# The sparse layer's counts are turned by transposing DMAs from SyncE instead of by TensorE

## The reference, cut to what matters

```python
inter = xf @ c1_w.T @ c2_w.T                      # 1792 columns
blk = inter.reshape(B * T, n_blocks, SPARSITY)    # 56 blocks of 32
idx = jnp.argmax(blk, axis=-1) + jnp.arange(0, INTER, SPARSITY)
h = jax.nn.relu(jnp.einsum('bkm,bm->bk', w1[idx], xf))
out = jnp.einsum('bk,bkm->bm', h, w2t[idx])
```

## Time and profile before

| what | value |
|---|---|
| median of 3 runs | 672.27 us (671.7 to 673.28) |
| the profiled execution's own time | 671.89 us |
| its span in the profile | 670.1 us |
| TensorE matmul busy | 638.2 us (95%), 3078 instructions |
| VectorE busy | 449.9 us (67%) |
| ScalarE busy | 213.8 us (32%) |
| GpSimd busy | 233.0 us (35%) |
| DMA | 40.66 MB, mean 61 GB/s |
| first layer's chunks (TensorE's bodies), about | 45 to 126, 145 to 226, 246 to 327, 346 to 428 us |

### The profile page before, as it was taken

One profiled execution on the slowest core, in us unless ns is written; L12 is line 12 of the kernel. 1 busy time (PEld: TensorE's weight loads), 2 busy tenths in 40 slices (PEclk: granted clock), 3 DMA queues, 4 the chain that ended last, 5 costly groups with the idle time before them and its releaser, 6 DMA issues.

```text
span 670.1 us, 8639 instructions
## 1 busy us (share of the span) xinstructions
PE 638.2 (95%) x3078; PEld 515.8 (77%) x3078; DVE 449.9 (67%) x716; ACT 213.8 (32%) x379; POOL 233.0 (35%) x185
## 2 busy tenths in 40 slices
PE   2599999999999999999999999999999999999997
PEld 2478788778788778788777788787878878887887
DVE  6977875597664597664597786664856667485633
ACT  2423333412122412122411233654146126413610
POOL 1516555360000360000390343464514342342441
PEclk9899999999999999999999999999999999999999
DMA  8940000040000040000052110013021013002001
GB/s 237 405 172 1 0 1 0 24 166 1 0 1 0 23 167 0 0 0 0 19 213 108 63 49 15 16 49 126 32 102 56 1 47 141 0 31 80 17 23 41
DMA packets 19535, 40.66 MB, mean 61 GB/s; under 512 B 2032, under 2 KB 2416, under 8 KB 18864
## 3 DMA queue, kind: packets, MB, share of 16 engines
q1 hardware_dynamic: 19504, 40.25, 16.9%
HBM read 31.85 MB, written 8.39 MB: 60 GB/s over the span
## 4 chain that ended last, share of the span: by engine, by line
PE 85%; DVE 8%; issue 3%; POOL 1%; ACT 1%; DMA 1%; SPq 0%; DVEq 0%; POOLq 0%; ACTq 0%
PE bank L410 76%; PE bank L344 2%; PE bank L1154 2%; PE bank L1135 1%; DVE counts L882 1%; DVE eq L872 1%; DVE seg_top L870 1%; PE bank L1286 1%; DVE ws_lo L935 1%; PE bank L1117 1%; PE bank L1249 1%; DMA x_tile<-in_x 1%; DVE h_lo L906 1%; POOL g_tile L390 1%; DVE ws_raw L930 1%
## 5 line engine op out<-in xcount | busy, mean ns | idle before, releaser
L410 PE MATMUL bank<-w_hi_t,h_hi 128*128 128x512 f32 x224 | 93.6, 418 | 1.5 <-DVE h_lo L906 1.5
L708 ACT ACTIVATE h_hi<-h 128x512 fp32r<-128x512 f32 x56 | 35.4, 632 | 176.4 <-DVE h L897 176.4
L882 DVE TENSOR_TENSOR_SCAN counts<-restart,eq 128x512 bf16<-128x512 bf16 (+1 forms) x64 | 87.4, 1365 | 2.0
L410 PE MATMUL bank<-w_lo_t,h_hi 128*128 128x512 f32 x224 | 87.9, 392 | 0.0
L410 PE MATMUL bank<-xT_hi,w_hi_t 128*128 128x512 f32 x224 | 87.6, 391 | 0.0
L410 PE MATMUL bank<-w_hi_t,h_lo 128*128 128x512 f32 x224 | 87.5, 390 | 0.0
L410 PE MATMUL bank<-xT_lo,w_hi_t 128*128 128x512 f32 x224 | 87.2, 389 | 0.0
L410 PE MATMUL bank<-xT_hi,w_lo_t 128*128 128x512 f32 x224 | 87.2, 389 | 0.0
L870 DVE TENSOR_REDUCE seg_top<-bank 128x16 f32<-128x512 f32 (+1 forms) x64 | 39.6, 619 | 67.8 <-PE bank L1135 67.8
L390 POOL TENSOR_TENSOR g_tile<-g_tile,s_tile 128x512 f32<-128x512 f32 x31 | 43.7, 1408 | 94.3 <-DVE g_tile L919 49.4
L376 POOL TENSOR_TENSOR rstd<-mean_var,eps 128x4 f32<-128x4 f32 x8 | 1.6, 202 | 173.9 <-DVE mean_var L370 173.9
(11 more groups left out here) (185 smaller groups left out, 1304.8 us busy)
## 6 DMA issues: line engine op xcount, KB each, us to landing
w_raw<-in_w SPq DMA_DIRECT2D x28, 256.0 KB, 9.5
x_res<-in_x SPq DMA_DIRECT2D x4, 1024.0 KB, 8.0
mid_state<-g_tile SPq DMA_DIRECT2D x16, 256.0 KB, 2.0
x_tile<-mid_state SPq DMA_DIRECT2D x4, 1024.0 KB, 7.4
x_res<-mid_state SPq DMA_DIRECT2D x4, 1024.0 KB, 5.5
out<-g_tile SPq DMA_DIRECT2D x15, 256.0 KB, 2.0
x_tile<-in_x SPq DMA_DIRECT2D x3, 1024.0 KB, 5.4
b_raw<-in_lora_b SPq DMA_DIRECT2D x2, 1024.0 KB, 4.9
```

What stands on the lines that cost most here:

```text
L410: last = nc.tensor.matmul(dst, a, b, start=(start and n == 0), stop=(stop and n == len(mms) - 1))
L708: nc.scalar.activation(h_hi[:, it % 2, :], h[:], ACT.Copy).then_inc(h_hi_done, 1)
L882: nc.vector.tensor_tensor_scan(counts[:, p % 2, tt, 0:PW[p]], restart[:, 0:PW[p]], eq[:, 0:PW[p]], 0.0, ALU.mult, ALU.add).then_inc(sel_co ...
```

## The change

The four transposes of each iteration leave TensorE. Behind each select's scan, SyncE waits for the count and issues one transposing DMA, from `counts` to a tile `first` in SBUF with the columns on its partitions. One DMA turns one row tile of a whole piece (128 rows by 512 or 256 columns of bf16), so there are 16 in a chunk and 64 in all, in place of 224 transposes. The mask reads `first` from SBUF, and waits at iterations 0, 4, 8 and 12 for the four DMAs of its piece. `counts` keeps one buffer per row tile, `first` has two. In the head each select now stands directly behind its own `s` product, and the fourth select moves from the body (behind up product 0) into the head. In SyncE's program the loads take places between the DMAs of the pieces.

```diff
+            def turn(c, p, tt):
+                sp.wait_ge(sel_count, c * NSEL + p * TT + tt + 1)
+                sp.sem_inc(turns, 1)
+                sp.dma_start_transpose(first[:, p % 2, 0:PW[p] // P, rows(tt)], counts[:, tt, 0:PW[p]])\
+                    .then_inc(ld_first[tt], 16)
...
             def chunk(c, source, last):
+                for tt in range(TT):
+                    turn(c, 1, tt)
                 sp.wait_ge(xT_tr, c * TT + TT)
                 sp.dma_start(x_tile[:], source).then_inc(ld_x, 16)
                 sp.dma_start(x_res[:], x_rows[c]).then_inc(ld_res, 16)
                 if last:
                     sp.wait_ge(s0_done, CH * TT)
                     sp.dma_start(wqkv_raw[:], wqkv).then_inc(ld_wqkv, 16)
                     sp.dma_start(a_raw[:], a_w).then_inc(ld_wqkv, 16)
                     sp.wait_ge(s_biased, CH * TT)
                     sp.dma_start(bias_a[:], bo.rearrange("(a n) -> a n", a=1).to_broadcast([P, D])).then_inc(ld_bo, 16)
+                for tt in range(TT):
+                    turn(c, 2, tt)
+                if last:
                     sp.wait_ge(up_done, (CH - 1) * IT + KD + 1)
                     sp.dma_start(base_raw[:], base_w).then_inc(ld_base, 16)
                     sp.dma_start(wo_raw[:], wo).then_inc(ld_base, 16)
...
+                for tt in range(TT):
+                    turn(c, 3, tt)
+                    if last and tt == 0:
+                        next_b(0)
+                if last:
+                    next_b(1)
+            def rows_out(c, place, to_next):
+                for tt in range(TT):
+                    if to_next:
+                        turn(c + 1, 0, tt)
+                    store_row(c, place, tt)
...
             def select_count(c, p, tt):
-                if tt == 0 and p >= 2:
-                    dve.wait_ge(first_tr, c * IT + 4 * (p - 1))
+                turned = c * PIECES + p
+                if not (isinstance(turned, int) and turned == 0):
+                    dve.wait_ge(ld_first[tt], turned * 16)
...
-                    dve.wait_ge(first_tr, c * IT + it + 1)
-                    nc.vector.scalar_tensor_tensor(h[:], first, 1.0, h[:], ALU.is_equal, ALU.mult).then_inc(h_masked, 1)
+                    if it % 4 == 0:
+                        for tt in range(TT):
+                            dve.wait_ge(ld_first[tt], (c * PIECES + it // 4 + 1) * 16)
+                    nc.vector.scalar_tensor_tensor(h[:], first[:, it // 4 % 2, it % 4, :], 1.0, h[:],
+                                                   ALU.is_equal, ALU.mult).then_inc(h_masked, 1)
...
-            def transpose_counts(c, it):
-                pe.wait_ge(sel_count, c * NSEL + (it // 4 + 1) * TT)
-                if it:
-                    pe.wait_ge(h_masked, c * IT + it)
-                for tt in range(TT):
-                    last = nc.tensor.transpose(first[:, rows(tt)], counts[:, it // 4 % 2, tt, rows(it % 4)], ident_bf[:])
-                last.then_inc(first_tr, 1)
...
-                s_product(c, 0)
-                s_product(c, 1)
-                select(c, 0, 0)
-                s_product(c, 2)
-                select(c, 0, 1)
-                s_product(c, 3)
-                select(c, 0, 2)
+                for tt in range(TT):
+                    s_product(c, tt)
+                    select(c, 0, tt)
```

More of the change, by code:

```diff
@@ L101, in block_mask_ffn_then_attention_lora_kernel @@
         ident = few.take("ident", [P, P])
-        ident_bf = few.take("ident_bf", [P, P], BF16)
         restart = few.take("restart", [P, BANK], BF16)
@@ L192, in block_mask_ffn_then_attention_lora_kernel @@
         eq = span_t.take("eq", [P, BANK], BF16)
-        counts = span_t.take("counts", [P, 2, TT, BANK], BF16)
+        first = span_t.take("first", [P, 2, TT, S], BF16)
+        counts = span_t.take("counts", [P, TT, BANK], BF16)
         h = span_t.take("h", [P, S])
@@ L268, in block_mask_ffn_then_attention_lora_kernel @@
         sel_count = sem("sel_count")
-        first_tr = sem("first_tr")
+        turns = sem("turns")
+        ld_first = [sem(f"ld_first_{tt}") for tt in range(TT)]
         up_done = sem("up_done")
@@ L416, in block_mask_ffn_then_attention_lora_kernel @@
         on = g_tile[:, 0, 2 * P:3 * P]
-        c2_f = counts[:].bitcast(F32).rearrange("p a t n -> p (a t n)")[:, 0:INTER]
+        c2_f = first[:].bitcast(F32).rearrange("p a t n -> p (a t n)")[:, 0:INTER]
         C2_PARTS = [slice(0, BANK), slice(BANK, INTER)]
@@ L422, in block_mask_ffn_then_attention_lora_kernel @@
         mask_bank = banks[5]
-        first = banks[7][:].bitcast(BF16)[:, 0:S]
         NSEL = PIECES * TT
@@ L463, in _, with store_row, next_b @@
                 sp.dma_start(bqkv_col[:], bqkv.rearrange("(j p) -> p j", p=P)).then_inc(ld_l1_small, 16)
+            def turn(c, p, tt):
[3 more added lines that the diff above has]
+                    .then_inc(ld_first[tt], 16)
+            def store_row(c, place, tt):
+                sp.wait_ge(rows_done, c * TT + tt + 1)
+                sp.dma_start(place[:, tt, :], g_tile[:, tt, :]).then_inc(st_rows, 16)
+            def next_b(i):
+                part = slice(i * KE // 2, (i + 1) * KE // 2)
+                sp.wait_ge(down_done, (CH - 1) * IT + part.stop)
+                sp.dma_start(b_raw[:, part, :], lora_b[:, part, :]).then_inc(ld_b[i], 16)
             def chunk(c, source, last):
+                for tt in range(TT):
+                    turn(c, 1, tt)
                 sp.wait_ge(xT_tr, c * TT + TT)
@@ L494, in _ @@
             sp.sem_inc(g_free, 1)
+            for tt in range(TT):
+                turn(0, 0, tt)
             with sp.Fori(0, CH - 1) as c:
                 chunk(c, x_rows[c + 1], False)
+                rows_out(c, mid_rows[c], True)
             chunk(CH - 1, mid_rows[0], True)
+            rows_out(CH - 1, mid_rows[CH - 1], False)
             def chunk(c, source):
@@ L525, in _ @@
             gp.memset(ident[:], 0.0).then_inc(consts_gp, 1)
-            gp.memset(ident_bf[:], 0.0).then_inc(consts_gp, 1)
             gp.memset(neg_half[:], -0.5).then_inc(consts_gp, 1)
             gp.memset(eps[:], EPS).then_inc(consts_gp, 1)
-            gp.wait_ge(consts_gp, 4)
-            for m in (ident, ident_bf):
-                gp.affine_select(out=m[:], in_=m[:], compare_op=ALU.not_equal, fill=1.0, base=0,
-                                 pattern=[[-1, P]], channel_multiplier=1).then_inc(consts_gp, 1)
+            gp.wait_ge(consts_gp, 3)
+            gp.affine_select(out=ident[:], in_=ident[:], compare_op=ALU.not_equal, fill=1.0, base=0,
+                             pattern=[[-1, P]], channel_multiplier=1).then_inc(consts_gp, 1)
             gp.sem_inc(s_free, TT)
@@ L886, in head @@
                 t_rest(c)
-                for tt in range(TT - 1):
+                for tt in range(TT):
                     select(c, 0, tt)
             def body(c, last):
-                select(c, 0, TT - 1)
                 for it in range(IT):
@@ L1178, in body @@
                     up_product(c, 0)
-                    select(c, 0, 3)
                 for it in range(1, IT + 1):
```

12 lines of the change are left out of this document (3 added, 9 removed).

## The result

The changed kernel takes 695.15 us (median of 4 runs, 694.8 to 697.05) beside 672.58 for the kernel before: ratio 1.0342, 95% interval 1.0321 to 1.0363, so 22.6 us slower. The direction was forecast; the forecast of 683.0 lies 12 us under the time, and the stated range holds it. The profiled execution took 697.05 us with a span of 694.9, 24.8 more than before.

The account below looks back on a forecast made before the run. TensorE, with 85% of the chain of waits, was taken to bound the kernel. Terms -13.5 + 1.5 + 2.3 + 2 + 7.0 + 7.2 + 1.7 + 3 = +11.2 on 671.89 gave 683.1 us; range 668 to 702.

Parts of the forecast that it names:

- term 3: Chunk 0: later opening, +2.3 us, and the mask with both operands in SBUF held by GpSimd, +2 us.
- Term 4: Last chunk: wqkv and a load behind a turn, so h_lo is late for down product 4, +7.0 us.
- Term 6: Last chunk: second half of b loads behind the turn of (3, 3), wanted in iteration 12, +1.7 us.
- Term 7: TensorE's clock at half speed after the long waits of terms 4 and 5, +3 us.
- Term 1: TensorE's transposes removed: 0.30 us for each of 45 groups, -13.5 us.
- Term 2: Openings of chunks 1 to 3: the turn's latency makes each about 0.5 us longer, +1.5 us.
- L: The turn, from a scan's end over SyncE's wait, issue and landing to the mask's start; taken as 4.0 us.
- rival (b): Openings: a turn as short as a store, L = 2.0, 8 us better, 675 us; chance 0.14.
- Term 5: Last chunk: base and wo load behind the turn of (2, 3), making TensorE wait in iteration 7, +7.2 us.
- Opening of the last chunk: Part of Term 2: one of three openings forecast about 0.5 us longer.
- What counted as nothing: No cost from x_tile and x_res of chunks 0 to 2, or turns of pieces 1 to 3 within an iteration.
- Rival (c): Last chunk: moved weights are hidden, terms 4 to 7 (18.9 us) fall away, faster at 663 us; chance 0.12.

Follow-up runs that it names:

- e7: Changed kernel with the last chunk's loads ahead of the turns and chunk 0 alone turned by TensorE into PSUM: 662.6 us.
- e1: Changed kernel with the last chunk's loads moved back ahead of the turns in SyncE's program: 673.0 us.
- e11: Kernel before with only the opening's order changed, each select right behind its s product: 667.8 us.
- e4: Kernel before with its mask reading unturned counts in SBUF instead of the turned counts in PSUM; TensorE still transposes: 682.7 us.
- e5: Changed kernel with its mask reading a PSUM bank filled once, not the counts; DMAs and waits stay: 680.4 us.
- e8: Kernel before with wqkv, a, bias, base, wo and b issued as late as in the changed one, x_tile and x_res early: 681.0 us.
- e9: Kernel before with every load of the last chunk, x_tile and x_res included, issued as late as in the changed kernel: 687.9 us.
- e2: Changed kernel with only the turns of piece 1 moved behind x_tile, x_res, wqkv, a and bias: 683.8 us.
- e3: Changed kernel with only the turns of piece 2 moved behind base and wo: 685.4 us.
- e12: As e7, with a second transposing DMA of 128x128 into an unread tile ahead of each turn: 674.4 us.

## Why the prediction came out as it did

The sign was right, and the mechanisms that the sum names all occurred; only half of the loss was forecast. The step that failed is term 3, chunk 0. It let GpSimd take 0.3 us from the mask in each of some eight iterations, +2 in all, and put the body's end at nothing. The runs showed a mask held to the end of GpSimd's instruction, 7.1 us over seven iterations, and 3 more at the body's end: +10. Terms 4, 6 and 7 were mis-sized as well: 9.0, 5.1 and 5.6 us where 7.0, 1.7 and 3 stood. Terms 1 and 2 were too pessimistic.

By chunks, chunk 0 was 9.3 us worse than forecast and the last one 8.0 worse, while chunks 1 and 2 together were 3.4 better. Without this last error the time would stand at about 698.6, an estimate from the table above. That lies in the range too, but the range's upper end was built of a longer L and a microsecond or two in each wait, and not of what came in chunk 0: that it holds the time is luck in part.

**Term 1 (-0.30 an iteration): 0.35.** 5.67 instead of 6.02. The matmul ahead of the transposes' place and the first behind it now start 0.23 apart. The 0.30 was put together from the rows of one group, and the period shows 0.05 more.

**Term 2 (L = 4.0, +0.5 an opening): L = 2.56, -0.9.** From rank product to down product 0 are 23.5 us in chunk 1, 24.4 before. The term's formula held: 247.4 + 2.56 makes 250.0 for the earlier trace rows, and 0.9 less than 250.93 is that. L was bounded rightly, and its value chosen too near the upper end: the turn landed 2.3 us after its issue (median), near the store's 2.0, and so near rival (b)'s condition of 2.0. The Trainium skill's 1309 ns for one 128x128 block (VectorE: DVE Perf Modes, The three transpose paths) had given 5.2 us for four; the trace doesn't bear that sum out, with 2.56 from scan to mask for all four blocks. Its advice (Rules for kernel authors) to leave a transpose with TensorE where PSUM will do holds in chunk 0 (e7 against e1) and not in chunks 1 and 2 (95.6 against e11's 99.1).

**Term 3 (+2.3 opening, +2 mask): +3.1 and +10.** The opening came out near its size by parts that were off both ways: L was 2.94 and not 4.0, while the scan ended 1.2 us later and the mask took 1.37. For the body the prediction named the cause and gave it a fraction of its price. The mask took 1.72 and not 0.66, and seven iterations 0.67 more each instead of 0.35 less: 7.1 us over an undisturbed body. Another 3 came at the body's end. The row that gave the price was in the earlier trace rows: a scan of 1.22 that took 4.27 beside GpSimd. In these rows an instruction with both operands in SBUF waits until GpSimd's, begun earlier, has ended, however much of it is left. The Trainium skill says so (SBUF — State Buffer, SBUF: two separate sides: the one that starts first has the shared pair "for the whole instruction"), and the rows agree, with ends at 64.18 and 64.74. e4 and e5 show the operand as the cause from both sides. The end of the body was not in the sum at all. TensorE, GpSimd and VectorE there in chunk 0, then the same work of GpSimd in the kernel before, and TensorE's wait in e4:

```profile
128.03 0.63 PE L345 MATMUL bank<-ident,x_tile 128*128 128x128 f32 x4 [3.21 <-DVE x_tile L385]
```

```profile
119.36 6.67 POOL L588 TENSOR_TENSOR s_tile<-s_tile,bias_a 128x512 f32<-128x512 f32 x4
```

```profile
127.33 1.92 DVE L385 TENSOR_SCALAR x_tile<-x_tile,mean_var,rstd 128x512 f32<-128x512 f32 x4 [2.42 <-POOL rstd L379]
```

```profile
110.33 5.86 POOL L561 TENSOR_TENSOR s_tile<-s_tile,bias_a 128x512 f32<-128x512 f32 x4
```

```profile
124.09 0.63 PE L344 MATMUL bank<-ident,x_tile 128*128 128x128 f32 x4 [2.00 <-DVE x_tile L384]
```

GpSimd adds `s` for 6.67 us ahead of `rstd`, 5.86 before. Two things make TensorE wait for it. In e5, with the iterations at 5.58 and the mask's operand in PSUM, 1.37 us of wait stay; in e4, with the iterations as before and the operand in SBUF, the wait is 2.00; both together make about the 3.21. In e1 it is 3.17, so it is not `x_tile`'s load.

**Term 4 (+7.0): +9.0.** From down product 3 to 4 are 16.74 us instead of 7.75. The chain was the predicted one: `a` at S + 11.8 forecast and S + 13.6 measured, then ScalarE, `wqkv_lo`, and `h_lo` of 3.50 us. The turn's issue takes 1.2 us where 0.7 stood for wait and issue together, and the string of loads took 12.3 us from the issue of `x_tile` to the start of ScalarE's rounding where 10.5 stood. That the string includes `x_tile` and `x_res` was right, and decides: e8, without them in it, has a wait of 1.38, and e9, with them, 7.49.

**Term 5 (+7.2): +6.5.** `h_lo` ends 9.5 us after the scan, forecast 10.0.

**Term 6 (+1.7): +5.1.** ScalarE's wait for the load is 2.4. The string behind it was not followed: `b_hi` late, `h_lo` late, and only behind that VectorE's norm of `x_tile` for which TensorE's row transposes wait (2.91), and then the clock again (the last products lie 6.03 apart for 3.66).

**Term 7 (+3): +5.6.** The periods behind the two long waits are 8.29 and 8.60 instead of 5.67 and 5.58. The clock did fall to 0.50. The estimate let that last 3.0 us, as the rows at hand showed it; here it went on from 387.0 until about 392, and half of some 5 us is 2.6.

**Opening of the last chunk: +1.4** where +0.5 stood (in e2, e3 and e7 it is 2.2 us shorter): mask 0.94 and `h_lo` 1.43 beside GpSimd.

**What counted as nothing** was right for the turns of pieces 1 to 3 (e12: doubled, iterations stay) and for `x_tile` in chunks 0 to 2 (e1: those chunks move by 0.9 at most). Rival (c) was right that early weights would take terms 4 to 7 away, but with the loads early the time is 673.0 and not its 663: chunk 0 stays 9.3 us longer than before. e7, which takes that away too, stands at 662.6, on (c)'s number by another sum, with the opening's order in it.

The sum by these measures: chunk 0 +10.0, chunks 1 and 2 -9.6, last chunk +24.7.

## What to carry to other kernels

When an operand moves from PSUM to SBUF, look at what GpSimd runs at that place and price each meeting at the rest of GpSimd's instruction, not at a fraction of VectorE's short one. When waiting instructions enter a DMA queue, write out for every load behind them what it waits for now and what stands ahead of it in bytes; here a reorder of one queue was worth 22 us. Measure a gain separately for each stage: turning by DMA gave 3.4 us in each of two chunks and under 1 in the fourth, and cost 7.5 to 10 in the first; left out of the first, and with the loads early, it made 662.6 of 673.3, of which the order of the opening alone gives 5.5.
